# Two unused 128-column products behind every TensorE group from the last score group of a two-layer vision tower on

## The reference

```
h = h + attn0(layernorm(h))      # causal, 16 heads, weights quantised to few levels
h = h + tanh(layernorm(h) @ W @ A1 @ A2 + b)
h = h + attn1(layernorm(h))      # not causal, with biases, 16 heads
h = h + moe(layernorm(h))        # 16 experts, top 1, capacity 76, 256 -> 1024 -> 256
```

## Time and profile before

| | |
|---|---|
| median of 3 runs | 414.4 us (413.15 to 415.01) |
| the profiled execution | 414.65 us, span 412.7 us |
| mean granted clock of TensorE | 0.915 |
| busy, share of the span | TensorE 85%, its weight loads 70%, VectorE 48%, GpSimdE 42%, ScalarE 39% |
| last score group | 262.46 us from the span's start |
| last products of the last `cnt` group | 288.59 us |
| first transposes of the expert inputs | 297.48 us |

### The profile page before, as it was taken

One profiled execution on the slowest core, in us unless ns is written; L12 is line 12 of the kernel. 1 busy time (PEld: TensorE's weight loads), 2 busy tenths in 40 slices (PEclk: granted clock), 3 DMA queues, 4 the chain that ended last, 5 costly groups with the idle time before them and its releaser, 6 DMA issues.

```text
span 412.7 us, 9288 instructions
## 1 busy us (share of the span) xinstructions
PE 351.9 (85%) x3412; PEld 287.3 (70%) x3412; DVE 199.2 (48%) x618; ACT 162.3 (39%) x441; POOL 173.8 (42%) x298
## 2 busy tenths in 40 slices
PE   3979898939998799996998596995199999999984
PEld 2857686837787488875787475774098888687872
DVE  0577625635774254763757388676113323123220
ACT  1559744324554366653664254434022222011210
POOL 0338835463773847555663675555100010100101
PEclk9969999968999699998999699686579999999998
DMA  8999111101026364234231122231499569898600
GB/s 255 409 428 434 44 37 47 45 15 43 30 88 175 92 199 155 84 113 156 86 93 62 46 68 65 78 117 38 143 371 364 212 202 373 302 356 342 210 8 11
DMA packets 38427, 66.00 MB, mean 160 GB/s; under 512 B 3939, under 2 KB 29478, under 8 KB 37552
## 3 DMA queue, kind: packets, MB, share of 16 engines
q1 hardware_dynamic: 33424, 55.70, 39.4%
q10 hardware_dynamic: 2448, 7.48, 4.7%
q0 software_dynamic: 2512, 2.25, 1.9%
HBM read 54.45 MB, written 8.48 MB: 152 GB/s over the span
## 4 chain that ended last, share of the span: by engine, by line
PE 57%; DMA 10%; issue 9%; SPq 8%; POOL 8%; ACT 3%; DVE 3%; ACTq 1%; POOLq 0%; DVEq 0%
PE bank L964 15%; PE bank L977 10%; SPq L650 8%; PE bank L856 7%; DMA early<-in_xt 6%; PE bank L903 4%; PE bank L884 3%; PE bank L917 3%; PE bank L892 3%; PE bank L866 3%; PE bank L924 3%; POOL rs L713 3%; DMA early<-vt 2%; PE bank L841 2%; PE bank L832 1%
## 5 line engine op out<-in xcount | busy, mean ns | idle before, releaser
L964 PEld LDWEIGHTS bank<-mid,early 128*128 128x128 f32 x512 | 60.6, 199 | 3.7 <-issue 2.8
L964 PE MATMUL bank<-mid,early 128*128 128x96 f32 x512 | 62.1, 283 | 0.6 <-ACT mid L1106 0.6
L762 POOL DMA_INDIRECT out<-mid,idx x12 | 11.7, 979 | 105.3 <-DVE mid L1275 105.3
L1115 ACT ACTIVATE mid<-bank,cols 128x96 f32<-128x96 f32 x64 | 16.6, 342 | 75.5 <-PE bank L964 75.5
L977 PE MATMUL bank<-early,mid 128*64 128x256 f32 (+1 forms) x448 | 43.7, 381 | 1.2 <-DVE mid L1292 1.2
L724 POOL TENSOR_TENSOR mid<-mid,tab 128x608 f32<-128x608 f32 x32 | 39.2, 1231 | 6.3 <-PE bank L884 5.5
L856 PE MATMUL bank<-xnT,attn 128*128 128x228 f32 (+1 forms) x192 | 38.8, 356 | 1.8 <-ACT vt L1076 1.5
L1206 DVE TENSOR_REDUCE mx<-bank 102x16 f32<-102x608 f32 x32 | 25.0, 783 | 31.3 <-PE bank L884 30.9
L903 PE MATMUL bank<-mid 114*38 114x51 f32 (+3 forms) x768 | 29.9, 224 | 11.3 <-issue 9.5
L903 PEld LDWEIGHTS bank<-mid 114*38 114x38 f32 (+1 forms) x768 | 26.9, 133 | 17.4 <-issue 13.6
L1292 DVE TENSOR_SCALAR mid<-bank,cols 128x96 f32<-128x96 f32 x64 | 15.9, 310 | 46.2 <-PE bank L964 36.4
(11 more groups left out here) (123 smaller groups left out, 617.5 us busy)
## 6 DMA issues: line engine op xcount, KB each, us to landing
early<-in_w SPq DMA_DIRECT2D x60, 512.0 KB, 8.0
v3a<-vt SPq DMA_DIRECT2D x102, 38.0 KB
early<-vt SPq DMA_DIRECT2D x90, 38.0 KB
expert_in<-k_empty SPq DMA_DIRECT2D x1, 3084.0 KB, 37.4
attn<-in_w SPq DMA_DIRECT2D x4, 512.0 KB, 8.6
mid<-expert_in SPq DMA_DIRECT2D x6, 257.0 KB, 6.0
mid<-expert_in ACTq DMA_DIRECT2D x6, 257.0 KB, 6.2
early<-in_xt ACTq DMA_DIRECT2D x1, 1536.0 KB, 28.9
```

The lines of the kernel that those rows point to most:

```text
L964: ins = mm(Hp[b][:, c // 4, (c % 4) * ECOLS:(c % 4 + 1) * ECOLS], w1s[e % SLOTS][:, kc, c * 128:c * 128 + 128], xeT[:, e, kc, :], start=kc ...
```

## The change

Behind every group of TensorE's list, from the last score group of the second layer on, two products of the 128x128 matrix of ones by the 128x128 identity are written to the first 128 columns of the two score banks, which nothing reads. Behind the score group itself TensorE first waits for the signal that VectorE has read the scores. 30 groups have two such products behind them, 60 in all.

```
                     ins.then_inc(full, 1)
+                if done.get("s", 0) == 2 * PAIRS:
+                    if kind == "s":
+                        pe.wait_ge(p_ready, 2 * PAIRS)
+                    for x in range(2):
+                        mm(Sp[:, x % 2, 0:128], ones[:, :], ident[:, :], start=True, stop=True)
```

## The result

The changed kernel takes 422.34 us (median of 4 runs, 422.05 to 425.24) against 413.77 us (median of 4) of the kernel before, a ratio of 1.022 with a 95% interval of 1.017 to 1.027. A second measurement with other runs of both gave 422.31 against 414.39 us, 1.018 (1.013 to 1.022). The forecast was 422.4 us.

A forecast was written before the change was run, and what follows sets the result against it. TensorE was taken to bound the router's end, with everything behind the last `cnt` in series. Last `proj` 8.9 us later, less 0.9 up to the last `cnt`, gives +8.0 and 422.4 us; range 419.5 to 426.5.

The forecast's parts named there:

- The wait: Behind the last score group, TensorE waits for VectorE's subtraction of row maxima; all 1.8 us exposed.
- The price of a pair: Two inserted products cost 0.44 us at full clock and 0.80 at half, priced from expert products and `proj`.
- From the wait to the last `proj`: Pairs add time, clock rises near 270.5 us; last `proj` begins 8.9 us later, including the wait.
- The late rise: Rival: clock rises at about 274 us instead of 270.5, sum +9.7 us; chance 0.24 shared with clock falling back.
- forecast case: Whole kernel: +8.0 us, 422.4 us, own range 421 to 424; chance 0.50.
- The last ten pairs: Last `proj` to last `cnt`: 4.4 us of pairs mostly covered by 4.6 us of waits; together -0.9 us.
- the pairs keep the clock up: Between last `proj` and last `cnt`, the last products take half their roughly 2.6 us at half clock: -1.3 us.
- Behind the last `cnt`: Slots, scatter, read back and the 8.5 us TensorE gap unchanged; experts only move: 0, 1 us either way.
- The rival with the other sign: Products hold full clock from the stretch's start, worth 3.65 us, further 3.6 at the experts, before product costs; chance 0.03.

The follow-up runs named there:

- second execution: Unaltered changed kernel, an execution profiled in the second measurement against the kernel before: 422.55 us, span 420.7 us.
- profiled one: Unaltered changed kernel, the execution profiled in the first measurement against the kernel before: 425.24 us, span 423.3 us.
- 16-column variant: Changed kernel with its wait and 60 products, but only 16 columns moving over the same 128x128 weights: 440.09 us, 1.064 against the kernel before.
- only the late pairs: Kernel before plus pairs only behind the 11 groups from the last `proj` group on, without the wait: 412.36 us, 0.998.
- that with the gap filled: Kernel before plus pairs from the last `proj` group on, no added wait, and 26 unused products behind the last `cnt`: 413.62 us, 0.997.
- moved wait: Changed kernel with the wait and first three pairs together behind `pt` 14 instead of the wait behind the last score group: 421.44 us, 1.013 against before.

## Why the prediction was right

- **The wait**, forecast at 1.8 us: 1.75 us of idle time in the second execution and in most variants, 2.16 in the profiled one, where the score group ran at full clock and TensorE stood still sooner.
- **The price of a pair**, forecast at 0.44 and 0.80 us. Taken alone a pair took 0.44 to 0.56 and 0.90 to 1.01, at half clock more than the upper side of the prediction (0.90); the groups between gave back part of it. Set down together, `ot` and its pair take 1.24 us at half clock (266.35 to 267.59) where 1.20 was counted, and the fifteen groups with their fifteen pairs at full clock take 15.2 us in the second execution (271.62 to 286.82) where the working has 15.4. So the term is right as what a pair adds. The neighbour L964 was the right row: the 16-column variant still costs 0.76 us at half clock.
- **From the wait to the last `proj`**, forecast 20.6 us: 20.3 in three executions (in the second the clock rose at 270.8), 22.8 where it rose at 274.9. The late rise was a rival with +9.7 us, and the profiled execution is that rival (+10.1). The medians of both measurements fit the forecast case. That the clock rises near 270.5 was assumed from the kernel before, and behind the wait alone it rose at 277.6, so the time of the rise was met rather than worked out. One reading behind it was wrong: the prediction has TensorE at half clock from 258.38 on, but the row of the kernel before has the clock at 1.0 until about 260.2, so that it fell while TensorE was busy, 1.8 us behind the wait, and stayed low for 10.3 us and not for 12:

```profile
260.00:261.00 1.00, 1.00 (x25) 1.00 (x24) 0.87 (x3) 0.00 (x0) 0.14 (x1) 0.61 0.19 61
```

- **The last ten pairs**, forecast as covered: 10.5 us for the stretch in both executions against 11.35 before, and leaving them out changed nothing (1.018 and 1.018). But the reasons given for the 0.9 us of gain did not hold as they stand. The larger was that the pairs keep the clock up (-1.3 us), and the stretch is as short (10.5) without them and with the clock falling in it. With only the late pairs it took 10.5 us in one execution and 11.2 in that with the gap filled. The size of this term is luck, and what shortened the stretch stays open.
- **Behind the last `cnt`**, forecast as unchanged: the idle time before the transposes is 7.9 us beside one more pair, and the experts started at half clock again. The clock rose 8.5 us (profiled) and 5.6 us (second) behind the first transposes, where 7.1 was before. Half of the difference, 0.7 us longer and 0.7 shorter, lies inside the 1 us either way that the forecast left open.
- **The rival with the other sign** had a sound mechanism and the wrong place. With unused products in the gap before the experts the array was at full clock when they started, and the kernel was 2.6 to 3.4 us faster; the prediction put an early clock there at 3.6. Inside the stretch where TensorE sets the time, the pairs' own 0.45 us each outweighs it. Of this rival's sums one is a little off: by its own terms (29 pairs of 0.44 us, less 3.65 for the clock and 5.2 of waits) it comes to +3.9, not +3.7.
- **The split between wait and products** was not tested by the total. The prediction has 1.8 us for the wait and so 6.2 for the products. Alone the wait costs 2.1 us by the ratio and 2.7 by medians, of which its one profile shows 1.8 of standing still and 1.7 of late clock (3.5 in that execution), and the products add some 5 to that. So the products cost less, and the wait more, than the sum has them, by up to 1 us each way; part of the agreement is luck. The expectation written for the wait alone (1 to 1.5 us) was too small, and so was the share of the wait in it. How much the clock adds to the wait on average is not settled: the moved wait differs from the change by 1.4 us, inside the intervals.

## What to carry to other kernels

Here unused products paid only where the engine would stand still and where the next work was bound by its clock; in the stretch that the engine itself bounds, they cost what its waits and an earlier rise of the clock did not give back, and from two to four products nearly their full time. Price an inserted product from the nearest real one with the same stationary shape and type, and ask separately what it does to the clock. Let a fill reach up to the work that it is meant for: products that pass at full clock take half the time, and in one execution the clock was lost again behind the 2.3 us that were left.

## What was not expected of the hardware

- TensorE was busy for 26.3 of 27.0 us, with products of 128 stationary and 16 moving columns between its groups, and stayed at 1.2 GHz, altogether from 254.4 to 329.5 us (with 7.6 us of idle time in it ahead of the transposes at 321.3).
- The clock fell inside waits of 2.16 and 1.27 us that began at full clock, and 2.1 us behind the end of one of 2.29 us; it held through one of 2.26 us with the same instructions around it.
- The same program's rises lay at 270.8 and 274.9 us in two executions, and the stretch around them differs by 2.5 us (20.3 and 22.8). Where the clock rose in the runs without a profile is not known.
